# A four-layer graph kernel on one core: masks ahead, transposed rows returned for the last layer, transposes in place of a join

## The reference, cut to what matters

```
def _L0(t, x, A):   Ax = A @ x
                    return 1.0 - 0.1 * x - 0.01 * sum(x * Ax, axis=1)
def _L1(x, adj, W): for k in range(2): x = tanh(concat([adj @ x, x]) @ W[k])
def _L2(x, adj, weight, bias):
    support = x @ weight
    mask = (adj != 0);  rank = cumsum(mask, axis=1);  deg = rank[:, -1:]
    k = minimum(deg, 100);  pos = rank - (deg - k)
    w = mask * where(pos > 0, 0.5 ** (k - pos), 0.0)
    return w @ support + bias
def _L3(X, t, Wt, B, W1, b1, W2, b2):
    u_intra = tanh(concat([X, t]) @ W1 + b1) @ W2 + b2
    XB = X @ B.T
    return u_intra + Wt @ XB - sum(Wt, axis=1) * XB
```

## Time and profile before

| | us |
|---|---|
| median of 3 runs | 795.0 (790.38 to 797.85) |
| the profiled execution | 788.66, span 786.6 |
| TensorE matmul busy | 714.9 |
| VectorE busy | 468.5 |
| ScalarE busy | 182.8 |
| GpSimd busy | 168.7 |

### The profile page before, as it was taken

The page is one execution under the profiler, slowest core; times in us unless marked ns, Lnnn a source line. Parts: engine busy times, 40 slices in busy tenths (PEclk is TensorE's granted clock), DMA queues, the critical chain, the costliest instruction groups (busy, mean ns, idle before and its releaser), DMA issues.

```text
span 786.6 us, 10295 instructions
## 1 busy us (share of the span) xinstructions
PE 714.9 (91%) x3752; PEld 287.1 (36%) x3752; DVE 468.5 (60%) x789; ACT 182.8 (23%) x279; POOL 168.7 (21%) x172
## 2 busy tenths in 40 slices
PE   1999999999899999999999967888888889999997
PEld 0333333333334333344444432333333333433333
DVE  5677666767988878555566625878888831111111
ACT  2000000000001000001010015777777731111111
POOL 5011110012000000012112232343454414222231
PEclk9999999999999999999999987999999999999999
DMA  9799999999999999999999948888999979999994
GB/s 372 312 423 420 421 419 420 421 418 366 345 387 408 385 383 374 379 358 359 362 370 367 350 192 330 328 309 316 341 349 339 330 247 373 351 369 369 367 367 191
DMA packets 48659, 280.96 MB, mean 357 GB/s; under 512 B 5985, under 2 KB 15329, under 8 KB 15713
## 3 DMA queue, kind: packets, MB, share of 16 engines
q1 hardware_dynamic: 38754, 271.39, 88.6%
q10 hardware_dynamic: 9856, 8.92, 3.5%
HBM read 275.56 MB, written 4.73 MB: 356 GB/s over the span
## 4 chain that ended last, share of the span: by engine, by line
PE 51%; DMA 31%; DVE 8%; POOL 4%; issue 4%; ACT 1%; SPq 0%; ACTq 0%; DVEq 0%; POOLq 0%
PE accA L993 34%; DMA land<-adj_blocks 15%; DMA cache<-adj_blocks 8%; DMA uS<-counts 5%; PE spare L1025 4%; DMA xin<-x_rows 3%; PE accA L1036 3%; DVE uS L835 2%; PE nat L926 2%; PE tr L902 2%; POOL rstd L495 2%; PE spare L1008 1%; PE nat L922 1%; DVE uS L825 1%; PE nat L918 1%
## 5 line engine op out<-in xcount | busy, mean ns | idle before, releaser
L993 PE MATMUL accA<-land,X 128*64 128x512 f32 x1536 | 370.1, 600 | 10.7 <-DMA land<-adj_blocks 7.8
L825 DVE TENSOR_TENSOR uS<-uS,land 128x512 f32<-128x512 f32 x192 | 133.1, 693 | 65.4 <-DMA land<-adj_blocks 56.1
L993 PEld LDWEIGHTS accA<-land,X 128*64 128x64 f32 x1536 | 103.0, 137 | 187.6 <-issue 136.2
L835 DVE TENSOR_SCALAR uS<-land 128x1024 bf16<-128x1024 f32 (+1 forms) x192 | 134.2, 747 | 53.6 <-DMA land<-adj_blocks 52.6
L993 PE MATMUL accA<-cache,X 128*64 128x512 f32 x512 | 126.5, 602 | 15.2 <-DVE X L867 12.5
L502 POOL TENSOR_TENSOR hS<-tS 128x256 f32<-128x256 f32 x32 | 25.6, 802 | 475.5 <-DVE tS L706 475.5
L407 ACT ACTIVATE wS<-spare 128x1024 uint16<-128x1024 f32 x112 | 108.6, 1033 | 56.2 <-PE spare L1025 56.0
L1025 PE MATMUL spare<-uS,triA 128*128 128x512 bf16 x256 | 78.5, 389 | 30.7 <-DMA uS<-counts 11.0
L1036 PE MATMUL accA<-wS,X 128*128 128x512 bf16 x256 | 77.7, 386 | 0.0
L583 ACT ACTIVATE rowsT<-tr 128x256 f32<-128x256 f32 x40 | 15.4, 385 | 236.2 <-PE tr L902 236.2
L993 PEld LDWEIGHTS accA<-cache,X 128*64 128x64 f32 x512 | 36.6, 138 | 83.2 <-issue 76.9
(11 more groups left out here) (78 smaller groups left out, 465.8 us busy)
## 6 DMA issues: line engine op xcount, KB each, us to landing
land<-adj_blocks SPq DMA_DIRECT2D x240, 1024.0 KB, 7.6
cache<-adj_blocks SPq DMA_DIRECT2D x16, 1024.0 KB, 12.3
xin<-x_rows ACTq DMA_DIRECT2D x32, 128.0 KB, 5.5
x_rows<-zS ACTq DMA_DIRECT2D x24, 128.0 KB, 5.0
cache<-x_rows SPq DMA_DIRECT2D x1, 1024.0 KB, 4.9
loadjS<-adj_blocks SPq DMA_DIRECT2D x64, 8.0 KB
uS<-counts SPq DMA_DIRECT2D x64, 4.0 KB
out_rows<-zS ACTq DMA_DIRECT2D x8, 128.0 KB, 7.3
```

Source lines behind the costliest of these rows:

```text
L825: nc.vector.tensor_tensor(total, total, of[:, i * W:(i + 1) * W], ALU.add)\
L835: nc.vector.tensor_scalar(masks(b)[0:rows, :], block_of(p, c, b)[0:rows, :], 0.0, None, ALU.not_equal)\
L993: last = nc.tensor.matmul(accA[k * D:(k + 1) * D, c % 2, :], tile(X[p % 2], TQ * b + k), of[:, k * W:(k + 1) * W], start=(b == 0), stop=(b ...
```

## The change

Load order in L0: the two cached pairs of chunk 1 are loaded before pair 6 of chunk 0. Masks in L2: four are made before the stage, and then mask b + 4 at block b; VectorE's relu of a block comes one block later rather than three. The leftover weights are made in L0 by VectorE and ScalarE for both counts of a tile, go through DRAM, and GpSimd's `left_over` is gone; L1044 contracts over 64 rows. The row sums move to columns 256 to 259 of `nat`, ahead of that step's other matmuls, and TensorE's waits at the heads of L1B and L2 change. L2's transposed rows are stored from `rowsT` and read back for L3, where layernorm and transposes are gone. In L3 four transposes take the place of the join, and VectorE adds the even and the odd part from PSUM.

```diff
+L0_LOADS = [(c, k) for c in range(NC) for k in range(PAIRS)]
+for _k in cached_pairs(1):
+    L0_LOADS.remove((1, _k))
+    L0_LOADS.insert(L0_LOADS.index((0, 6)), (1, _k))
...
+LEAD = 4
-EVAC_LAG = 3
+EVAC_LAG = 1
-HT_PE = {L1B: 5, L2: 6}
+HT_PE = {L1B: 5, L2: 7}
-ROW_STAGES = {"rows": 0, "centre": 2, "variance": 3, "norm": 5, "transpose": 5, "transposed": 9, "hidden": 9,
-              "tanh0": 13, "tanh1": 14, "intra": 15}
+ROW_STAGES = {"rows": 0, "hidden": 2, "tanh0": 5, "tanh1": 6, "intra": 9}
+ROW_STAGES_0 = {"rows": 9, "hidden": 9, "tanh0": 12, "tanh1": 13, "intra": 15}
-         L3: {0: 1, 1: 1, 2: 3, 4: 3, 5: 5, 6: 6, 7: 10, 8: 12}}
-SUM_STAGES = {"sums": 3, "summed": 7, "result": 11, "store": 13}
+         L3: {0: 1, 1: 1, 2: 3, 4: 3, 5: 5, 6: 6, 7: 8, 8: 10}}
+SUM_STAGES = {"sums": 3, "result": 7, "store": 11}
...
-        sums_p = spare[:, 0, 0:4]
+        sums_p = nat[:, CH:CH + 4]
```

On SP:

```diff
+            def left_adjacency(c):
++                if c:
+                    sp.wait_ge(left_later, c)
+                else:
+                    sp.wait_ge(cleared, 1)
+                sp.dma_start(loadjS[1:2 * NT:2, :], left_in_d[:, c * W:(c + 1) * W]).then_inc(left_adj, 16)
             def left_over(c):
+                if c >= 2:
+                    sp.wait_ge(weighed, c - 1)
+                sp.dma_start(left_weights(c), left_d[c]).then_inc(left_in[c % 2], 16)
+            def left_rows_of(c):
+                sp.wait_ge(cleared, 1)
+                sp.wait_ge(copy_used, copied_no(L1B, c, 1) + 1)
+                for t in range(4 * c, 4 * c + 4):
+                    sp.dma_start(loS[2 * t + 1:2 * t + 2, :], tile16(t)[LAST:P, :]).then_inc(left_rows, 16)
+            def keep_rows(c):
+                sp.wait_ge(tr_evac, tr_no(L2, c) + 1)
+                sp.dma_start(hT_d[c], rowsT[:, :]).then_inc(hT_out, 16)
+            def rows_back(c):
+                sp.wait_ge(hT_out, 16 * (c + 1))
++                if c < 2:
+                    sp.wait_ge(w_used, NQ * NC - WRING + c + 1)
+                else:
+                    sp.wait_ge(hidden_done, c - 1)
+                sp.dma_start(hidden_rows(c), hT_d[c]).then_inc(hT_in[c % 2], 16)
             def after_masks(g):
+                if g >= 2 * PAIRS and g % PAIRS == 2:
+                    keep_rows(g // PAIRS - 2)
...
+                if g in (1, 3, 7):
+                    left_rows_of({1: NC - 3, 3: NC - 2, 7: NC - 1}[g])
...
-                    left_over(0)
-                    after_masks(0)
+                    sp.wait_ge(left_out, 16 * NC)
+                    left_over(0)
+                    left_over(1)
+                    after_masks(-1)
...
+                    if p == L0 and k == 7 and c:
+                        left_adjacency(c - 1)
+                    if p == L3 and c == 0 and k == 5:
+                        rows_back(0)
+                        rows_back(1)
+                        keep_rows(NC - 2)
+                    if p == L3 and c == 1 and k == 5:
+                        keep_rows(NC - 1)
+                    if p == L3 and c >= 2 and k == 1:
+                        rows_back(c)
+                    if p == L1B and c >= 3 and k == 2:
+                        left_rows_of(c - 3)
```

On ScalarE, in L0 behind the store of the counts, and in L2 ahead of the copy to `rowsT`:

```diff
+                    nc.scalar.activation(loweightS, lolaterS, ACT.Relu, bias=wt("full", rows=(0, D)),
+                                         scale=-BIT * BIT).then_inc(left_made, 1)
+                    act.dma_start(left_d[c], loweightS).then_inc(left_out, 16)
+                    if p == L2 and c:
+                        act.wait_ge(hT_out, 16 * c)
```

On VectorE, in the last step of L0's epilogue, in L3's `result`, in `main` and in `step`:

```diff
+                        dve.wait_ge(left_adj, 16 * (c + 1))
+                        nc.vector.scalar_tensor_tensor(out=lolaterS, in0=loadjS, scalar=0.0, in1=countS,
+                                                       op0=ALU.is_equal, op1=ALU.max).then_inc(left_later, 1)
+                        parts = nat[:, :].rearrange("p (t h d) -> p h t d", h=2, d=D)
+                        L(nc.vector.tensor_tensor(rows4(tS), rows4(side), parts[:, 0], ALU.add))
+                        nc.vector.tensor_tensor(rows4(zS), rows4(tS), parts[:, 1], ALU.add).then_inc(nat_evac, 1)
+                if p == L2 and NQ * c + b + LEAD < NQ * NC:
+                    mask(p, (NQ * c + b + LEAD) // NQ, (b + LEAD) % NQ)
                 if p == L2 and b - EVAC_LAG in EVAC_DVE:
                     weights_out(dve, nc.vector, c, b - EVAC_LAG)
...
+                if p == L2 and c == 0:
+                    for b in range(LEAD):
+                        mask(p, c, b)
```

On TensorE:

```diff
+                    elif p == L3:
+                        for j in range(4):
+                            last = nc.tensor.transpose(nat[:, j * P:(j + 1) * P], accS[:, j * P:(j + 1) * P],
+                                                       wt("ident"))
-                if p == L1B and c == 0:
+                if p == L2 and c == 0:
                     pe.wait_ge(count_ready, NC)
-                if p == L2 and c == 0:
-                    pe.wait_ge(rowsum_ready, NC)
-                        pe.wait_ge(left_rows, 32)
+                        pe.wait_ge(left_rows, 16 * NT)
```

## The result

Median of the changed kernel 769.1 us (four runs) against 795.7 before (four runs); ratio 0.966, 95% interval 0.959 to 0.973. One of the four, 1218.8 us at a mean granted clock of 0.56, counts in that median and is left out of the ratio; the other three took 765.9 to 770.1. The profiled execution took 768.10 us (span 766.3), 20.3 us of span less. The medians differ by 26.6: the execution of the kernel before that was profiled, at 788.66 us, is faster than each of its four timed runs (790.4 to 797.9).

What follows compares the result with a forecast made beforehand. It took L0 as DMA-bound, L2 as TensorE waiting on counts, masks and row sums, L3 as TensorE-bound. Terms -2.5, -7, -15.7, -1.4 and -5.1 sum to -31.7 us: 795.0 to 763, range 750 to 780.

Steps and rivals of the forecast that it cites:

- Rival B: Everything opens: L2 chunks of 17.1 us, entry -12, cheap transposes, L0 -5; 747 us, chance 0.12.
- rival C: L2: VectorE's relus of blocks 4 and 12 come late and stop TensorE; slower from 2.4 us per wait; chance 0.03.
- rival D: L3: returned rows arrive late, the hidden layer waits; +5.1 us instead of -5.1, 775 in all; chance 0.11.
- Entry to L2: Last L1B chunk's work at L2's start: earlier first triangle, partly lost to later waits; -7 us, bounds -3 and -12.
- three links: Entry to L2: three counts loads ahead, four masks made before the stage, row sums moved into nat; first triangle at 463.3.
- L2: The other seven chunks of L2: 18.0 us each instead of 20.25, -15.7 us, bounds -22 and -7.4.
- Step (b): L2: mask lead of four and more blocks keeps VectorE's stage work from delaying TensorE's next mask; part of -15.7 us.
- Step (a): L2: removing GpSimd's left_over speeds masks by 0.3 us each in part of the chunk; part of -15.7 us.
- Step (c): L2: relu of block 4 or 12 stands behind a later mask, but VectorE is further ahead; no separate size.
- Rival A: L2 stays tied to its transfers, counts loads waiting for ring slots; chunks 19.2 us, -7.4, 772 us; chance 0.22.
- L0: L0: reordered loads fill a DMA gap, -5.0 us; added loads and stores cost +2.5; sum -2.5, bounds -5 and 0.
- L3: L3: fewer transposing matmuls, -5.1 us; join replaced at no change; a wait before first-chunk transposes goes, -1.4.

Runs made afterwards that it cites:

- e8: Kernel before the change with one edit: three counts loads instead of four ahead of L2's first loads; 790.8 us, ratio 0.989.
- e5: Changed kernel with the earlier mask schedule (no mask lead, relus three blocks later, transposes back at block 13); 796.8 us, ratio 1.001 to the kernel before.
- e9: e5 with L2's load of the old rows issued at block 11 of the chunk itself instead of block 1 of the next; 779.7 us, ratio 0.981.
- e7: Changed kernel with three idle 32x512 operations per chunk of L2 put back on GpSimd; 767.5 us, ratio 0.962.
- e12: Changed kernel with all 16 relus of a chunk of L2 on ScalarE, none on VectorE; 765.6 us, ratio 0.967.
- e3: Changed kernel with L0's loads back in their plain order; 771.8 us, ratio 0.968.
- e4: Changed kernel where only chunk 0 of L0 loads leftover adjacency and stores leftover weights, 14 transfers of 64 KB left out; 766.9 us, one run.
- e13: Changed kernel with L1B's 20 row copies moved to ScalarE's queue and the row sums behind the step's other matmuls; 770.4 us, ratio 0.970.
- e16: Changed kernel with the edits of e13 and e12, and L2's old rows loaded at block 11 of the chunk itself; 764.8 us, ratio 0.964.
- e6: Changed kernel with L3's join, ScalarE's copy and one add in place of four transposes and two adds; 768.9 us, one run.

## Why the prediction was right, and where its terms were off

The time, 769 against 763, lies in the range. It comes closer than the stages do: the table misses the forecast by 11.4 us and the medians by 5.1, since the kernel before happened to be profiled in a short execution. That the median lies so near is in this part luck. But the reading of the profile held where most of the time was: L2 and its entry lost their gaps, L3 lost TensorE work, and the waits for counts, masks and row sums went. Rival B falls with the chunks of L2, the entry and L0, and rival C with waits of 8.1/6 = 1.4 us for VectorE's relus where it needed 2.4; no wait for the returned rows shows in L3 (rival D).

**Entry to L2**: -4.9 for -7, by the first of its three links. SP's fourth counts load was the cause (e8), while the masks made ahead were no part of it (e5); the wait moved to the transposes as foretold (3.8 us where I had 5), the row copies cost 1.4 us (I had 2), and the clock dropped behind the wait (0.50 from 478 to 482), which I had only as a bound.

**L2**: -13.9 for -15.7, chunks 18.27 for 18.0. The size was right and the cause in part wrong. Step (b), the mask lead with the settings that go with it, is the term: without it nothing is left of the change (e5), though a good third of what L2 lost in e5 goes with a lower clock, so the term's size isn't read from it. And its work is to cover a wait of VectorE for the old rows, not the work of the layernorm (e9). Step (a), GpSimd's operations, was worth nothing with the mask lead in place (e7); without the lead it wasn't tried. Step (c) was waved through and is what remained: 8.1 us of relus late on VectorE, and 0.6 us per chunk when they move away (e12). Rival A, transfers as the bound of L2, is out by the same run, and with it the reading of a DMA share of 0.99 as a limit. The 370 to 384 GB/s of L2 also lie above the 358 that the prediction took from the Trainium skill ("DMA: Bandwidth & Descriptors", "Where 436 GB/s comes from"), so its floor of 19.0 us per chunk does not hold in this kernel: the trace has 18.27, and 17.64 in e12.

**L0** is the step that failed: -2.5 forecast, +1.9 measured. The load order was priced at the whole gap of the DMA, 5.0 us, in a stretch where TensorE was busy 20.3 of 20.3 us in the very row that shows the gap. What comes in early can't be used early: the second chunk ended 1.4 us earlier and the next stretch moved less (386 GB/s for 423). In its own comparison the order was worth 1.3 to 2.6 us (e3). The added bytes were priced at 0.31 us per chunk by the rate of the large loads and cost 0.6 (e4), and from 60 to 180 us the stage moved 414 GB/s where it moved 420 before and again in e4. They move in pieces of 1 and 2 KB; whether that is why was not tested. The +1.9 of the table is itself at the low end: with 186.2 us for the mean of the kernels at full clock, L0 lost 2.6.

**L1B** was priced at nothing and took 3.3 us more. I had followed SP's queue in L2 only; the row copies in L1B hold it for 2.4 to 3.6 us per chunk. And the row sums, moved ahead of the step's matmuls, delay ScalarE's copy by their own 1 us and with it a layernorm chain whose end TensorE awaits: hS waits of 3.4 us for 1.1. Both are candidates. With the two taken back together L1B took 144.2 and 145.1 us (e13, e16), but e8, with the code of before, took 146.4, so neither part is shown by itself and the size of the whole is open.

**L3**: -7.2 for -6.5. The transposes proved cheaper than my middle value (0.59 for 1.07 us), which brought next to nothing (e6): below 17.0 us per chunk of TensorE work, waits for loads appear (from 660 to 762 TensorE's matmuls stand 1.5 us at them and its weight loads 6.2), a bound that I had ruled out by a rate, 402 GB/s.

## What to carry to other kernels

An idle resource is worth its gap only if the engine behind it was short of it in that same stretch: read both columns of the window before pricing. A wait can cost more than its length: where the granted clock fell behind waits, a chunk of the same work took 1 to 1.6 us more of TensorE (e5, e8, e13). In an engine's queue written by hand, a wait on a small DMA costs the work behind it; issue that DMA as soon as its buffer is free, or put independent work ahead of the wait, and don't expect both to pay. Follow each moved step through every stage in which it runs, also the stages that the change doesn't name.

## What the runs showed of the hardware that I had not expected

Four SBUF-to-SBUF copies of 256 bytes held SP's queue for 2.4 to 3.6 us; one took 0.50 to 1.73 us (median 0.59), against a median of 0.33 us for the issue of a 1 MB load into `land`. A 128 KB load of old rows, issued on ScalarE's queue while the 1 MB loads ran on SP's, took 7.3 to 8.3 us (the medians of the kernels of the changed kind; 5.5 before) from issue to landing, as long as a 1 MB load (7.5). An fp32 `transpose` of 128x128 ran as one instruction of 272 ns with a weight load of 140 (medians), where a plain fp32 product of that shape (L918 of the kernel before) takes two instructions of 275 ns with weight loads of 191.
